# An attention and feed-forward layer on one core: the order of value products and transpositions on TensorE

## What is computed

```
q, k, v = x @ wq + bq, x @ wk + bk, x @ wv + bv      # split into 8 heads of 48
attn    = softmax(q k^T * 48**-0.5 + adj)            # per head, 512 x 512
x1      = rmsnorm(x + (attn v) @ wo + bo)            # alpha1, gamma1
x2      = rmsnorm(x1 + silu(x1 @ w1 + b1) @ w2 + b2) # alpha2, gamma2
out     = layernorm(x + x2)
```

## Time and profile before

| | us |
|---|---|
| median of 3 runs | 1932.65 |
| lowest and highest | 1932.32, 1933.24 |
| the profiled execution | 1933.91 |
| its span, first to last instruction | 1932.1 |

### The profile page before, as it was taken

One profiled execution on the slowest core, in us unless ns is written; L12 is line 12 of the kernel. 1 busy time (PEld: TensorE's weight loads), 2 busy tenths in 40 slices (PEclk: granted clock), 3 DMA queues, 4 the chain that ended last, 5 costly groups with the idle time before them and its releaser, 6 DMA issues. The chain is left out here.

```text
span 1932.1 us, 39573 instructions
## 1 busy us (share of the span) xinstructions
PE 1893.6 (98%) x10336; PEld 1608.8 (83%) x10336; DVE 1332.8 (69%) x2579; ACT 1141.9 (59%) x2056; POOL 1127.9 (58%) x1739
## 2 busy tenths in 40 slices
PE   6999999999999999999989999999999999999998
PEld 5777777777877777777768999999999999999997
DVE  5777777777777777777876666656656655666645
ACT  3777777777787777777765444334444334444432
POOL 3655445654456544555667566667665766655643
PEclk9999999999999999999989999999999999999999
DMA  5545545555444554565533222112222112222001
GB/s 173 152 142 152 160 124 142 143 151 160 123 143 142 151 158 125 146 176 152 154 115 125 88 87 84 50 43 83 87 87 87 54 41 79 87 87 87 28 31 41
DMA packets 118732, 214.36 MB, mean 111 GB/s; under 512 B 19489, under 2 KB 47905, under 8 KB 116769
## 3 DMA queue, kind: packets, MB, share of 16 engines
q1 hardware_dynamic: 118688, 213.87, 36.3%
HBM read 108.93 MB, written 41.94 MB: 78 GB/s over the span
## 5 line engine op out<-in xcount | busy, mean ns | idle before, releaser
L982 DVE TENSOR_TENSOR pT_lo<-ps_t,pT_hi 128x512 fp32r<-128x512 f32 x512 | 348.9, 687 | 104.1 <-ACT pT_hi L780 102.9
L780 ACT ACTIVATE pT_hi<-ps_t 128x512 fp32r<-128x512 f32 x512 | 303.1, 596 | 153.4 <-PE ps_t L1221 145.1
L773 ACT ACTIVATE probs<-probs,neg_max 128x512 f32<-128x512 f32 x512 | 357.0, 721 | 34.5 <-DVE neg_max L975 33.4
L975 DVE CUSTOM_DVE_ANT_0 probs<-ps_s,adj_s 128x512 f32<-128x512 f32 x448 | 294.3, 683 | 58.8 <-issue 27.3
L1221 PE MATMUL ps_t<-ident,probs 128*128 128x128 f32 x2048 | 314.2, 277 | 12.3 <-DVE pT_lo L982 9.6
L1221 PEld LDWEIGHTS ps_t<-ident,probs 128*128 128x128 f32 x2048 | 243.1, 141 | 97.4 <-issue 40.5
L1715 DVE TENSOR_TENSOR h_lo<-hidden,h_hi 128x512 fp32r<-128x512 f32 x192 | 170.2, 887 | 172.4 <-ACT h_hi L1625 172.2
L651 POOL CAST tails<-k_wide 16x512 fp32r<-16x512 f32 x384 | 233.4, 608 | 50.6
L647 POOL CAST k_wide<-k_wide 32x512 fp32r<-32x512 f32 x128 | 78.2, 611 | 315.2 <-DMA k_wide<-weights_hi 291.5
L1814 PE MATMUL ps_y<-w_hi,h_hi 128*128 128x384 f32 x768 | 258.2, 336 | 0.0
L1814 PE MATMUL ps_y<-w_hi,h_lo 128*128 128x384 f32 x768 | 257.0, 335 | 0.0
(11 more groups left out here) (114 smaller groups left out, 3963.2 us busy)
## 6 DMA issues: line engine op xcount, KB each, us to landing
ctx_dram<-ctx_stage SPq DMA_DIRECT2D x128, 224.0 KB
ctx_raw<-ctx_dram SPq DMA_DIRECT2D x15, 1792.0 KB, 7.3
q_wide<-weights_lo SPq DMA_DIRECT2D x192, 96.0 KB, 2.3
k_wide<-weights_hi SPq DMA_DIRECT2D x192, 96.0 KB, 2.4
adj_first<-in_adj SPq DMA_DIRECT2D x32, 512.0 KB, 6.5
adj_s<-in_adj SPq DMA_DIRECT2D x32, 512.0 KB, 6.4
rows<-in_xT SPq DMA_DIRECT2D x16, 768.0 KB, 4.9
rows<-in_x SPq DMA_DIRECT2D x16, 768.0 KB, 6.2
```

What stands on the lines that cost most here:

```text
L773: nc.scalar.activation(probs[:, at, :], probs[:, at, :], ACT.Exp, scale=-1.0, bias=neg_max[:, at:at + 1]).then_inc(exp_done, 1)
L780: nc.scalar.activation(pT_hi[:, h % 2, qt, :, :], ps_t[qt % 2][:, :].rearrange("p (k i) -> p k i", k=TT), ACT.Copy)\
L975: nc.vector.tensor_tensor_reduce(out=probs[:, at, :], in0=ps_s[qt][:, :], in1=rows, scale=-1.0, scalar=BIG, op0=ALU.add, op1=ALU.min, accu ...
L982: nc.vector.tensor_tensor(pT_lo[:, h % 2, qt, :, :].rearrange("p k i -> p (k i)"), ps_t[qt % 2][:, :], pT_hi[:, h % 2, qt, :, :].rearrange ...
```

## The change

In the stretches of heads 2 to 6, PE's list has `begin(h)`, a transposition, `end(h)`. The change puts `end(h)` straight behind `begin(h)`, and the transposition behind both. In four of the five places this is the fourth tile, in the stretch of head 3 it is the third, with the fourth behind it. The value products of heads 1 to 5 are then eight matmuls in a row; those of head 0 are so already, and those of heads 6 and 7 keep a transposition (head 7: two) in their middle. No other engine's list changes.

```
--- before.py
+++ after.py
@@ -1298,15 +1298,15 @@
                 scores(b, 3)
                 transpose_probs(b, 2, 2)
                 begin(1)
+                end(1)
                 transpose_probs(b, 2, 3)
-                end(1)
 
                 transpose_probs(b, 3, 0)
                 scores(b, 4)
                 transpose_probs(b, 3, 1)
                 begin(2)
+                end(2)
                 transpose_probs(b, 3, 2)
-                end(2)
                 transpose_probs(b, 3, 3)
                 projection("q0")
 
@@ -1316,8 +1316,8 @@
                 projection("k0")
                 transpose_probs(b, 4, 2)
                 begin(3)
+                end(3)
                 transpose_probs(b, 4, 3)
-                end(3)
 
                 transpose_probs(b, 5, 0)
                 scores(b, 6)
@@ -1325,8 +1325,8 @@
                 projection("q1")
                 transpose_probs(b, 5, 2)
                 begin(4)
+                end(4)
                 transpose_probs(b, 5, 3)
-                end(4)
 
                 transpose_probs(b, 6, 0)
                 scores(b, 7)
@@ -1334,8 +1334,8 @@
                 projection("k1")
                 transpose_probs(b, 6, 2)
                 begin(5)
+                end(5)
                 transpose_probs(b, 6, 3)
-                end(5)
 
                 transpose_probs(b, 7, 0)
                 if not last:
```

## The result

The changed kernel takes 1953.83 us (median of 4 runs, 1950.19 to 1956.62) against 1932.95 for the kernel before: a ratio of 1.0107, 95% interval 1.009 to 1.0123. It is slower by 20.9 us, where 13.6 were forecast. The sign was right, and so was the chain of heads 1 and 2; at head 5 the forecast followed a late result to the wrong reader, in the last batch it left terms out, and the time lies outside the range given. The profiled execution took 1950.19, its span is 1948.4.

A forecast was written before the change was run, and what follows sets the result against it. PE, busy for 98% of the span, was taken as the bound. Fourteen loop batches (12.7 us), the first (0.2) and the last (0.7) sum to 13.6, giving 1946.3 us, 0.7% slower; range 1939.3 to 1951.

The forecast's parts named there:

- the chain of heads 1 and 2: Head 2's fourth tile, transposed 0.91 us later, delays ACT and DVE until head 3's fourth transposition waits: 0.73 us a batch.
- head 5: Late copy of k1 delays VectorE's half of it, then the transposition of head 7, tile 2: 0.24 us a batch.
- the last batch: The already waiting fourth transposition of head 3 costs 0.7 us more; nothing is added for head 5.
- The saving on PE: Heads 1 to 5: fewer switches between products and transpositions save 0.03 us a head, 2.4 us at most.
- Heads 3 and 4: Margin of 0.22 us remains at the next heads' tile 1 transposition, so no wait; each head saves 0.03 us.
- Rival 3: Margins of 0.22 us prove too thin, tile 1 of heads 5 to 7 waits: 8.4 us added, chance 0.12.
- rivals 1 and 2: Either no wait comes, 0 to -2.4 us (chance 0.07), or the wait before head 3's first transposition goes, 7.5 gained (0.05).
- the signs named: About 45 PE waits for pT_lo instead of 15; eight products 1.92 us, tile pair 0.79, a batch 0.9 longer.
- The first batch: The 1.6 us wait for POOL takes up head 2's loss; head 5's 0.2 us is left.

## Why the prediction was right and wrong

- **The saving on PE, 0.03 a head: right, and too small to be told.** Heads 2, 3 and 4 together shorten a batch by 0.05 us and leave the time where it was (0.9991 to 1.001). The Trainium skill's 81 ns for a matmul of 128 columns ("TensorE: Matmul & The Clock Gate", Back-to-back issue gap) would have made it an estimated 0.14 a head. The trace does not agree with that figure: the pair of tiles took 0.79 us again, some 0.11 for each matmul of the second tile.
- **Head 1 and 2: right.** 0.73 forecast, 0.79 measured in the step 4 to 5. The chain was right link by link: from the start of T(2,3) to that of T(3,3) it took 310.34 - 304.10 = 6.24 us, and 306.03 - 299.79 = 6.24 were forecast. The difference is that T(2,3) stood 0.76 ahead of T(3,0) in place of 0.80, and that q0 came 0.38 behind T(3,3) in place of 0.36.
- **Heads 3 and 4: right**, no wait. Rival 3 did not come about, nor did rivals 1 and 2. Of the signs named, the list was to show about 45 waits for pT_lo; it shows 32, because T(7,2) has none in the loop.
- **Head 5: the step that failed.** I wrote that DVE's half of k1 would be late by 0.91 and followed it down DVE's list to lo(7,0) and T(7,2), at 0.24. I did not ask who else waits for that operation. It frees a bank: `use_before` gives q2 the bank of k1, and `wait_for_bank` makes PE wait for `proj_lo`. q2 stands 2.2 us ahead of T(7,2) on PE. The step measured 0.48 (7.25 to 7.73), double the term, and T(7,2)'s wait was covered by it. With the split of k1 put first, the step is 7.25 again.
- **The last batch: mis-sized**, 0.7 forecast, 2.0 measured, and head 5 costs 0.4 more in batch 14 than in the loop. Head 1 was put at 0.7 and cost 1.5: where T(3,3) waits already there is no margin, so 0.91 was the price of the delay alone, and that DVE's splits there would take longer is in no row I had. "Nothing for head 5" was wrong: in the last batch no scores of a next batch stand between T(7,0) and T(7,1), so the margin by which T(7,1) was safe in the loop is not there. It waits 1.07 and costs 0.93. Of the 2.4 for both heads some 0.4 does not show, as the granted clock was higher in this execution.
- **The first batch:** 0.2 forecast, 0.5 measured (head 5 again). The wait for POOL took up head 2's loss as forecast; it shrank from 1.6 to 0.4.
- **The sum** in one execution: 14 x 1.22 for the loop, 0.5 for the first batch, 0.4 for batch 14 and 2.0 for the last, 20.0 us by the steps, 19.8 by the start of the feed-forward phase, where 13.6 were forecast. Of the difference, 14 x 0.24 = 3.4 is the bank of q2, 1.3 the last batch, 0.4 head 5 in batch 14, 0.8 the step of head 2, 0.3 the first batch, and the rest small terms. Between these 20 us and the 20.9 of the medians stand differences between executions, of which the last section shows one.
- **The range** was built on 0.1 a wait of uncertainty in lags. The lags were good to 0.02. What was uncertain was whether I had every reader of the late results, and for that the range had no room.

## What to carry to other kernels

When an instruction is moved on the engine that bounds, list what becomes late behind it on the other engines, and for each late result look up every semaphore wait on it, those that only free a buffer or a bank too; the first reader in program order on the bounding engine sets the price. A place that shows no idle time may have a margin of 0.2 us, and the place that pays is often a head further on: here the loss was seen at head 2 and caused at head 1. In a tight order of three engines the cheap win was to move one copy or difference ahead of an independent operation on the slack engines (7 us), not to regroup the matmuls.

## What the runs showed of the hardware

Executions of one kernel differ by more than I had thought from three runs: the kernel before ran between 1928.84 and 1936.81 us in 22 executions on one chip, the change between 1950.19 and 1956.62 in 4. The profiled pair shows a source of it. In the first 40 us of the feed-forward phase (the columns are the stretch, its length, busy time of PE, PEld, DVE, ACT and POOL, the granted clock, DMA share, GB/s) the kernel before

```profile
1009.77:1049.77 40.00, 37.28 (x159) 31.76 (x160) 26.43 (x26) 25.18 (x39) 29.14 (x26) 0.91 0.49 166
```

and the change

```profile
1029.56:1069.56 40.00, 38.00 (x180) 32.58 (x181) 24.94 (x25) 24.63 (x38) 27.84 (x26) 1.00 0.49 166
```

The kernel before had the lower level, 1.2 GHz, for part of the stretch: 0.66 of full speed in its first 5 us, right behind an idle time of 2.70 us that both kernels have before the phase, and 0.91 on average. The change in this execution had the full 2.4 GHz throughout. An average of 0.91 over 40 us is 7.2 us at half speed, an estimated 3.6 us lost. The whole phase was 922.3 us before and 918.8 with the change, though not an instruction of it differs, and behind these 40 us the granted clock is 1.00 in both. So the profiled pair shows 16.3 us of loss where the start of the phase shows 19.8 and the medians 20.9. Times of a single execution are worth little here below 3 us; the steps between starts in the loop repeat to 0.02.
